# Key mask of the second attention layer: from a GpSimd sum into the score products of TensorE

## What is computed

```python
q = (xn @ Wq).reshape(b, n, H, DH).transpose(0, 2, 1, 3) * scale
kv = xn @ Wkv
sim = jnp.einsum('bhid,bjd->bhij', q, k)
bias = jnp.concatenate([null_col, attn_bias], axis=-1)
sim = sim + bias
...
# causal triangle and key mask: those entries become very negative
attn = jax.nn.softmax(sim, axis=-1)
out = jnp.einsum('bhij,bjd->bhid', attn, v)
return layernorm(out @ Wo, g_out)
```

## Time and profile before

| | |
|---|---|
| time, median of 3 runs | 1536.22 us (1531.81 to 1537.91) |
| time of the profiled execution | 1532.06 us |
| its span, first to last instruction | 1530.3 us |
| mean granted TensorE clock | 0.954 of full speed |
| busy: PE, PEld | 1341.0 us (88%), 1170.8 us (77%) |
| busy: DVE, ACT, POOL | 1130.7 us (74%), 884.1 us (58%), 810.9 us (53%) |
| layer "c" attention | about 640 to 997 us from the span's start |

### The profile page before, as it was taken

How to read it: one execution, slowest core, us unless ns; L and a number is a source line. 1 busy time by engine, 2 the same in 40 slices (tenths; PEclk the granted TensorE clock), 3 DMA queues, 4 the chain that set the end, 5 groups by cost and what they waited for, 6 DMA issues and landing times.

```text
span 1530.3 us, 43531 instructions
## 1 busy us (share of the span) xinstructions
PE 1341.0 (88%) x15534; PEld 1170.8 (77%) x15535; DVE 1130.7 (74%) x2217; ACT 884.1 (58%) x2209; POOL 810.9 (53%) x844
## 2 busy tenths in 40 slices
PE   1799999999669999989999999668997199999994
PEld 0689889898559999878888888557886178888883
DVE  4498888888834645789999998568883996445457
ACT  1566676766536666646656665347774165445544
POOL 1356665665414545465555554278873206777713
PEclk9999999999979999999999999979997599999997
DMA  7200000000130000000000000010002222232354
GB/s 203 42 28 9 8 9 9 8 9 8 32 82 1 1 0 0 1 10 9 7 9 9 9 8 13 19 50 15 14 15 90 89 87 74 96 96 97 92 183 157
DMA packets 89683, 65.04 MB, mean 42 GB/s; under 512 B 50862, under 2 KB 84401, under 8 KB 89522
## 3 DMA queue, kind: packets, MB, share of 16 engines
q1 hardware_dynamic: 82610, 44.98, 10.7%
q0 software_dynamic: 6912, 17.84, 3.7%
HBM read 39.18 MB, written 18.35 MB: 38 GB/s over the span
## 4 chain that ended last, share of the span: by engine, by line
PE 75%; DVE 11%; issue 5%; ACT 5%; POOL 1%; SPq 1%; DMA 0%; DVEq 0%; ACTq 0%; POOLq 0%
PE psW L1898 12%; PE psQ L1819 12%; PE psQ L2179 8%; PE psW L2161 5%; PE psS L1880 4%; PE psS L1923 4%; PE psT L1856 3%; PE psQ L1992 3%; PE psW L1980 3%; PE psM L1980 3%; PE psS L1992 3%; PE psM L1867 2%; PE psM L2153 2%; PE psT L2169 1%; PE psM L1837 1%
## 5 line engine op out<-in xcount | busy, mean ns | idle before, releaser
L712 POOL TENSOR_TENSOR pn<-ex,rden 128x1024 f32<-128x1024 f32 x64 | 144.6, 2259 | 244.1 <-PE psT L1856 239.5
L1819 PEld LDWEIGHTS psQ<-xT,wq 128*128 128x128 f32 x1536 | 196.6, 196 | 46.0 <-issue 24.1
L1898 PE MATMUL psW<-wout,oT 128*128 128x256 f32 x1536 | 210.2, 292 | 16.5 <-ACT oT L945 14.4
L1819 PE MATMUL psQ<-xT,wq 128*128 128x256 f32 x1536 | 216.5, 293 | 1.5 <-ACT cur L1026 1.5
L1898 PEld LDWEIGHTS psW<-wout,oT 128*128 128x128 f32 x1536 | 195.3, 194 | 29.3 <-ACT oT L945 24.0
L2179 PE MATMUL psQ<-W,exT 128*128 (+1 forms) x624 | 172.5, 412 | 0.1
L757 POOL TENSOR_TENSOR hT<-hf,hT 128x512 fp32r<-128x512 f32 x64 | 84.5, 1321 | 99.7 <-ACT hT L1022 99.7
L2179 PEld LDWEIGHTS psQ<-W,exT 128*128 128x128 f32 x624 | 110.9, 191 | 19.4 <-issue 0.4
L830 POOL DMA_INDIRECT rows<-xf,src x72 | 72.3, 1005 | 72.5 <-issue 57.3
L1322 DVE SCALAR_TENSOR_TENSOR oT<-psS,nvcol,oT 128x512 fp32r<-128x512 f32 x128 | 89.7, 740 | 24.0 <-ACT oT L945 23.5
L2161 PE MATMUL psW<-W,ehT 128*128 (+1 forms) x624 | 100.7, 297 | 5.7 <-DVE ehT L1758 5.7
(11 more groups left out here) (299 smaller groups left out, 3479.7 us busy)
## 6 DMA issues: line engine op xcount, KB each, us to landing
both<-results SPq DMA_DIRECT2D x16, 512.0 KB, 8.3
raw_w<-W SPq DMA_DIRECT2D x27, 256.0 KB, 4.8
vv<-vp SPq DMA_DIRECT2D x256, 16.0 KB, 1.8
xf<-xf_all SPq DMA_DIRECT2D x4, 1024.0 KB
out<-X SPq DMA_DIRECT2D x8, 512.0 KB, 2.9
X<-x SPq DMA_DIRECT2D x1, 3584.0 KB, 15.2
raw_q<-Wq SPq DMA_DIRECT2D x2, 1024.0 KB, 5.9
bvv<-v_all SPq DMA_DIRECT2D x128, 16.0 KB, 1.8
```

What stands on the lines that cost most here:

```text
L712: nc.gpsimd.tensor_tensor(pn[:], ex[t % 2][:, :, 0:S], rden[:].unsqueeze(2).to_broadcast([P, H, S]), ALU.mult).then_inc(sem("t_pn"), 1)
L1819: mm = nc.tensor.matmul(psQ[:, cc, h * QT:h * QT + QT], wq[w][:, k, c * P:c * P + P], xT[g % 2][u][:, k, :], start=(k == 0 and j == 0), st ...
L1898: mm = nc.tensor.matmul(psW[:, 0:D], oT[u][:, c, :], wout[w][:, c, :], start=(u == 0 and c == 0 and w == 0), stop=(u == 1 and c == CH - 1))
```

## The change

In layer "c", too, the key mask is written into the score banks by four bf16 products on TensorE. GpSimd's `masked` table and its 32 additions are gone. VectorE adds `bias_t` itself, in the pass that it made before with `masked`, and the null column now stands ahead of that pass. The mask words are laid out in SBUF as in layer "a", which takes four DMAs in place of two.

```diff
-        masked = sb("work", "masked_bias", [P, H, S], F32)
+        place["work"][0] += 4 * K
...
-        LOADED = {"a": 16 * 20, "c": 16 * 12}
+        LOADED = {"a": 16 * 20, "c": 16 * 14}
...
-                    if L["cosine"]:
-                        for half in range(2):
-                            row = half * S + b * (S // 2)
-                            sp.dma_start(mask_w[row:row + S // 2, :, :], seq.to_broadcast([S // 2, TILES, S // 4])).then_inc(ld, 16)
-                    else:
-                        sp.dma_start(mask_w[b * S:(b + 1) * S, :, :], seq.to_broadcast([S, TILES, S // 4])).then_inc(ld, 16)
+                    for half in range(2):
+                        row = half * S + b * (S // 2)
+                        sp.dma_start(mask_w[row:row + S // 2, :, :], seq.to_broadcast([S // 2, TILES, S // 4])).then_inc(ld, 16)
...
-                    if live(t) and not L["cosine"]:
-                        if t == 0:
-                            pool.wait_ge(sem("l_mask"), nth(L, "mask", 1))
-                        reach(pool, sem("t_sum"), done + t)
-                        nc.gpsimd.tensor_tensor(masked[:], bias_t[:], negmask[:, t:t + 1, :].to_broadcast([P, H, S]),
-                                                ALU.add).then_inc(sem("t_bm"), 1)
...
                         else:
-                            dve.wait_ge(sem("t_bm"), t + 1)
-                            nc.vector.tensor_tensor(by_slot(e[:, :, 0:S]), scores, by_slot(masked[:]), ALU.add).then_inc(sem("t_left"), 1)
                             nc.vector.tensor_tensor(e[:, :, S], sn[t % SN][:], nbias[:], ALU.add).then_inc(sem("t_null"), 1)
+                            if t == 0:
+                                dve.wait_ge(sem("l_causal"), nth(L, "causal", 2))
+                            nc.vector.tensor_tensor(by_slot(e[:, :, 0:S]), scores, by_slot(bias_t[:]), ALU.add).then_inc(sem("t_left"), 1)
                             dve.wait_ge(sem("t_left"), done + t + 1)
...
-                        if L["cosine"]:
-                            if t == 0:
-                                pe.wait_ge(sem("l_mask"), 1)
-                            for a in range(2):
-                                for b in range(2):
-                                    q = slice(b * S, b * S + S)
-                                    f = slice((a ^ b) * S, (a ^ b) * S + S)
-                                    nc.tensor.matmul(psS[q, a, :].rearrange("p (c j) -> p c j", j=S), pick[f, b, :],
-                                                     negmask[f, t:t + 1, :].to_broadcast([S, CH, S]),
-                                                     start=True, stop=False, skip_group_check=True)
+                        if t == 0:
+                            pe.wait_ge(sem("l_mask"), nth(L, "mask", 1))
+                        for a in range(2):
+                            for b in range(2):
+                                q = slice(b * S, b * S + S)
+                                f = slice((a ^ b) * S, (a ^ b) * S + S)
+                                nc.tensor.matmul(psS[q, a, :].rearrange("p (c j) -> p c j", j=S), pick[f, b, :],
+                                                 negmask[f, t:t + 1, :].to_broadcast([S, CH, S]),
+                                                 start=True, stop=False, skip_group_check=True)
...
-                                                          kT[f, q], start=not L["cosine"], stop=True, skip_group_check=True)
+                                                          kT[f, q], start=False, stop=True, skip_group_check=True)
```

## The result

The changed kernel took 1543.18 us (median of 11 runs, 1537.13 to 1545.86), the kernel before 1536.22 (11 runs, 1531.81 to 1537.91). The ratio is 1.0048, with a 95% interval of 1.0035 to 1.0061: slower by 5.4 to 9.4 us, at the edge of the 0.5% bound. The profiled execution took 1544.27 us, with a span of 1542.5 us at a mean granted clock of 0.949. Of all runs in this document one was slow (of e3: 1601.16 us at a clock of 0.82), and it is left out everywhere.

The account below looks back on a forecast made before the run. TensorE was taken to pace layer "c", with VectorE's lateness costing only 0.14 us a step. Terms +5.4, -3.6, -0.1, -1.0, +0.2 and +1.9 gave +2.8 us: 1534.9 by the profiled execution, 1539.0 by the median; forecast 1538, range 1530 to 1546.

Parts of the forecast that it names:

- +1 to +5 us: Whole kernel: the forecast band for the slowdown against the kernel before, given a chance of 0.60.
- A: Layer "c" steps: TensorE hides the four products behind the projection's tail; 5.6 us less, so -2.8 us; chance 0.08.
- C: Layer "c" steps: the four products cost 0.3 to 0.41 us, +6 to +9 us in all; chance 0.08.
- The sum: Whole kernel: steady, first and last steps of layer "c" together cost +2.8 us, or 0.2%.
- Four products a step, 0.20 us each: TensorE, layer "c": mask products add 0.20 us a step (bounds 0.18 and 0.41), +5.4 us over 27 steps.
- My estimate of 0.31: TensorE, layer "c": mask products' cost in us a step if the stated overhead adds to their columns; total +5.8.
- 0.14 us of TensorE's wait for `oT[1]` gone: Steady steps, layer "c": VectorE no longer late, so 26 projections lose 0.14 us each, -3.6 us.
- First steps -0.1: Layer "c"'s start: VectorE gains 0.1 us, not 2.3, as the null column and bias sum stand behind `pn`.
- Last steps -1.0 + 0.2 + 1.9 = +1.1: Layer "c"'s end: `oT[1]` wait gone -1.0, tile 30's scores +0.2, last null column behind `pn` +1.9 us.
- B: First steps and last tile: null column never stands behind `pn`; 2.2 + 1.8 us less, so -1.2 us; chance 0.12.
- D: Every step: null column stands behind `pn`, TensorE waits 1.3 us a step, 35 us, about 1573; chance 0.04.
- rival E: TensorE's granted clock, seen falling in the last steps: other gaps add or drop slow pieces, 1.5 to 3 us either way; chance 0.08.

Follow-up runs that it names:

- e3: Changed kernel with layer "c"'s key mask left out, so without the four mask products a step: 1537.97 us, ratio 1.0010 to the kernel before.
- e12: Kernel before, unchanged, run once more for its trace: 1540.47 us (one run).
- e1: Changed kernel, run again as it was: 1540.70 us, ratio 1.0032 to the kernel before.
- e9: Kernel before with filler products on TensorE in the last five steps of layer "c": 1530.88 us, ratio 0.9962.
- e7: Changed kernel with up to 27 filler products a step on TensorE in the last five steps of layer "c": 1537.29 us, ratio 1.0006 to the kernel before.
- e4: Kernel before with only the null column moved ahead of the bias sum, mask still on GpSimd: 1538.42 us, ratio 1.0015.
- e8: Kernel before with the null column ahead of the bias sum for tiles 3 to 30 only: 1532.49 us, ratio 0.9974.
- e2: Changed kernel with the null column put back behind the bias sum: 1537.50 us, ratio 1.0001 to the kernel before.
- e10: Kernel before with the null column ahead for tiles 3 to 30 and fillers in layer "c"'s last five steps: 1531.23 us, ratio 0.9957.

## Why the prediction was right, and where it was short

The time (1543.18) is inside the range (1530 to 1546), 5.2 us above the 1538.0 forecast. But the medians differ by 7.0 us, and the ratio gives 5.4 to 9.4: above the +1 to +5 us to which I gave 0.60. It is the width of the range, set by rivals A and C, that holds the time, and neither of these came: being inside is in part luck. What was right is the mechanism of each term. Here are four traces, the two lower ones with fillers, where no clock is lost in the last steps:

| trace | to "a"'s last PV | to "c"'s last projection | to the end |
|---|---|---|---|
| before again (e12) | 441.2 | 562.2 | 535.3 |
| changed again (e1) | 434.0 | 566.0 | 539.0 |
| before, fillers (e9) | 437.3 | 558.2 | 535.2 |
| changed, fillers (e7) | 436.0 | 561.3 | 537.2 |

**The sum held.** With the clock kept up, the change costs 561.3 - 558.2 = 3.1 us in the layer (0.65 in the first steps, 1.5 in the steady ones, 0.93 in the last); the sum was +2.8. One trace of each stands behind this. Its terms, one by one:

- Four products a step, 0.20 us each step: 0.17 to 0.19 by e3. The Trainium skill (TensorEngine Tiling (Array Packing), Instruction Overhead) states an overhead of about 60 cycles for each matmul. My estimate of 0.31 added it to the columns, and e3 does not bear this addition out.
- 0.14 us of TensorE's wait for `oT[1]` gone: the projections take 3.12 us, and a step is 10.25 us (10.26 forecast). By e4 and e8 this gain comes from the column's place alone, and needs no products.
- First steps -0.1: +0.14 between the first two traces and +0.65 between e9 and e7, with the column behind `pn` at tiles 1 and 2 (1.23 and 1.22 us), and 2.3 us lower in e2, where it stands behind the bias sum.
- Last steps -1.0 + 0.2 + 1.9 = +1.1: 0.93 (e7 against e9), with a column of 1.91 us behind the last `pn`. From PV product to PV product, the step with the last bias sum is 1.81 us longer in e7 (11.74 against 9.93), and the one whose projection had waited for `oT[1]` is 0.84 shorter (9.21 against 10.05). Who starts first decides: `pn` 0.45 us ahead costs the column 1.7 us, `pn` 0.06 us behind costs it nothing (e2). The Trainium skill (SBUF — State Buffer, Who interferes with whom) has this rule, and the rows agree.

A, B, C and D did not come: the products cost about what was taken, the columns stand where it was said, and nowhere else.

**What was short is the size of rival E.** I gave the clock 1.5 to 3 us either way, from the one slow projection of the earlier trace rows. Two things were wrong in this. First, the cost of the lower clock in the last steps is 5.2 us in the changed kernel (53.17 in e1 and 53.16 before it, against 47.99), and in the kernel before 1.2 us in one trace and 4.3 in another (48.24 and 51.34 against 47.06). One trace cannot give this term. Second, the parts with the same code scatter too: layer "a"'s last PV product came anywhere from 433.3 to 441.2 us. The 12.2 us between the two first spans are 2.6 of the change's own work (0.14 + 1.5 + 0.93), 4.0 more in the last steps (4.9 less 0.93), where projections ran at the lower clock, and 5.6 (4.4 + 1.2) in code that nobody changed.

**Is the clock in the last steps then why the medians differ by more than the sum?** I thought so after e7, and e9 took it away. The mean of the 18 runs of the changed kernel is 1541.8 us and that of the 73 runs of before 1536.2: 5.6 apart. With fillers they are 1537.1 (12 runs) and 1531.4 (8 runs): 5.7 apart. The fillers took 4.7 us from the one and 4.8 from the other (5.5 from each, if each group's mean is taken against the runs of the kernel before beside it). So the clock in the last steps costs both kernels about the same on average, and the difference between them stays when it is gone.

**What stays open** is the rest: by ratios 1.0006 less 0.9962 is 0.44%, 6.8 us (3.7 to 9.8 by the two intervals), and the traces of e7 and e9 show 3.1 of it. The mean granted clock of the runs does not differ (0.9507 over the 18 runs, 0.9510 over the 73). What the traces offer is the part behind layer "c", whose code is the same: 537.7 us on average in the seven traces of the changed kernel and its variants (534.4 to 539.2), 535.5 in the seven of the kernel before and its variants (534.7 to 537.6). These ranges overlap; 1.5 us of their scatter is the last projection itself, which takes 4.6 us in five of the fourteen traces and 3.1 in the others.

One piece of this part does not overlap: the experts' up-projection on TensorE, before and changed, with its first and last start:

```profile
L2179 PE MATMUL psQ<-W,exT x624: 387/397/775, 1219.8 to 1506.3; 128*128 x108, 128*128 128x512 f32 x48
...
L2170 PE MATMUL psQ<-W,exT x624: 387/397/776, 1230.7 to 1518.6; 128*128 x108, 128*128 128x512 f32 x48
```

That is 286.5 us before and 287.9 changed. In the seven traces of each kind it is 286.5 to 286.8 and 287.4 to 288.3, on average 1.3 us more with the change. The matmuls take the same time; TensorE stands idle ahead of the transposes of the gathered rows, with nothing in the profile that it waits for ("issue"), 2.8 to 3.2 us in all before and 3.8 to 4.8 changed. It is not the products (287.4 in e3, which has none), nor the column's place (286.5 in e4, 287.9 in e2), nor the fillers (286.7 in e9). What is left of the change is all that e3 and e2 keep of it: GpSimd's additions gone, the mask's other layout and its DMAs, and code that stands elsewhere. No run separates these. With 3.1 this makes 4.4 us of the 6.8, inside its interval; the cause of the 1.3, and where the rest lies, I leave open.

## What to carry to other kernels

Work moved from an engine that has slack to the one that sets the pace costs there what it adds to a step (0.18 us here, for products whose record lasts 0.41); before moving it, look whether the wait that it causes can be had by order alone. Here the place of one instruction of 0.2 us was worth the whole gain in the steady steps (0.9974 in e8), and it wants another place in the first and last steps than in the steady ones: where an instruction of VectorE and one of GpSimd met, the one that started first was not held (e2, e10). And where a difference of 0.3% is looked for, read the granted clock of two traces of the same kernel before explaining a difference between two kernels.

## What I had not expected of the hardware

Extra products that compute nothing make both kernels faster, by 4.7 us or more. In the last steps TensorE waits 1 to 4 us at several places, and projections of 4.6 us follow, part of each at 1.2 GHz; with the waits filled, the clock stays at 1.00 and they take 3.1 us. The busy time of such a stretch does not tell by itself where the clock falls. The kernel before, in two stretches of its last steps:

```profile
950.00:960.00 10.00, 7.28 (x113) 5.85 (x112) 8.80 (x10) 4.75 (x11) 5.01 (x2) 1.00 0.34 87
960.00:970.00 10.00, 7.44 (x155) 5.99 (x157) 7.35 (x10) 4.61 (x8) 5.01 (x2) 1.00 0.03 5
```

TensorE was busy 7.28 and 7.44 of 10 us at a clock of 1.00, and in the changed kernel 7.87 from 960 to 970 at 0.83. The same program's first 440 us differ by 7.9 us between two executions (433.3 and 441.2).
